# A cross-attention kernel's first microseconds: warm-up on ones from VectorE, first key weights in two halves

## The chip, the cores and the metric

The kernel runs on one core of a Trainium2 chip. The metric is the device time of one execution in microseconds. The core's engines are named as the profile names them: PE is TensorE's matmul part and PEld its weight loads, DVE is VectorE, ACT is ScalarE, POOL is GpSimd, SP is SyncE, and the names with a q (SPq, ACTq) are the queues on which an engine issues its DMAs.

## The reference

The layer updates 128 latent rows of width 256 in three steps, each added to x: cross-attention to 12544 context rows (16 heads of 64), self-attention with low-rank additions, and a linear layer on rows rounded to fp8. Nearly all work is in the first.

```python
def _L0_xattn_ref(latents, context, ln_l_w, ln_l_b, ln_c_w, ln_c_b, Wq, Wkv, Wo, bo):
    lat = layernorm(latents, ln_l_w, ln_l_b)
    ctx = layernorm(context, ln_c_w, ln_c_b)
    q = (lat @ Wq).reshape(b, n, H, D).transpose(0, 2, 1, 3)
    kv = ctx @ Wkv
    k, v = jnp.split(kv, 2, axis=-1)
    ...
    attn = jnp.einsum('bhnd,bhsd->bhns', q, k) * scale
    attn = jnp.clip(attn, -11.0, 11.0)
    attn = jax.nn.softmax(attn, axis=-1)
    out = jnp.einsum('bhns,bhsd->bhnd', attn, v)
    ...
    return out @ Wo + bo

x = x + _L0_xattn_ref(_layernorm(x, axis=-1), ctx_1024, ...)
x = x + _L0_attn_ref(_layernorm(x, axis=-1), ...)
x = x + _L0_ffn_ref(_layernorm(x, axis=-1), ...)
```

## The kernel before

The 12544 context rows are worked in 49 pairs of 128-row tiles, and the 16 heads in two passes of 8, so the middle of the kernel is twice 49 pairs. For each tile TensorE computes the scores of 8 heads from the context (transposed in its layout, its first column subtracted) and weights into which query, key weights and the layer norm's scale are folded, then the values, then the weighted sum. fp32 accuracy comes from pairs of a high and a low part (three matmuls each, lines 463 to 465). ScalarE takes exponentials and makes high parts, VectorE clips, makes low parts and adds denominators, GpSimd computes the roots for the norms.

Every engine runs its own list of instructions; order across engines is set by hand with semaphores, and each engine's list is in program order. A DMA is issued from SP's or ACT's list and raises its semaphore by 16 when it has landed.

The head, which the change touches, goes as follows.

- SP issues its loads in the order of lines 325 to 337: x, the second chunk of the first half of Wk, the first context pair, the first half of Wq, the first transposed pair, the second pair (lines 312 and 317), the second half of Wq, the first half of Wv, pairs three and four, the second half of Wk.
- ACT issues the column constants (line 799) and the first chunk of Wk's first half (line 800, 256 KB, semaphore wk_half0_loaded).
- POOL makes the identity (lines 402 and 403), then small constants, and later, behind the roots of the first three pairs, the row of ones, the square of ones `ones_sq` (line 429), a head mask and the ones of `av`. All raise `s_const`, on whose count others wait.
- DVE waits for the identity and the columns, makes the folding matrix `foldT` (lines 1092 to 1097), then the layer norm of x (to line 1104, which writes `lat`), then statistics and differences of the first pairs.
- TensorE waits for the identity, runs `keep_warm(9)`, nine fp32 matmuls of the identity with itself whose results nobody reads (line 566; the trace shows each fp32 matmul as two passes), then waits for foldT and for the first chunk of Wk and folds it (`key_fold`, line 533), transposes `lat` (line 576), folds the second chunk, computes the queries from Wq (`q_heads`, line 548), and goes on to the query-key products (line 555) and the first scores (line 463).

`ones_sq` is read otherwise only by `denominators`, where a tile's denominators are summed by query, at the end of each pass; in pass two TensorE waited for `s_const` of 4 ahead of it.

Of the kernel before, what the change touches and what calls it, by code (L numbers as in the profile page):

```python
# [17 lines left out]
P = 128  # L18
# [5 lines left out]
def perceiver_layer(  # L24
    nc, x, ctx, ctxT, cols, Wq, Wk, Wv, Wo, bo,
    aWq, aAq, aBq, aWk, aAk, aBk, aWv, abv, aAv, aBv, aWo, abo, aAo, aBo,
    f_weight, f_scale, f_bias, out,
):
    _, N, D = x.shape
    PAIRS = ctx.shape[0]  # L30
    H, DH = Wo.shape[1], Wo.shape[0]
# [14 lines left out]
    CM = MH // CH  # L46
# [9 lines left out]
    with ExitStack() as stack:  # L56
        def sb(name, shape, dt=F32):
            return stack.enter_context(nc.sbuf_tensor(name, shape, dt))

        def sem(name):  # L60
            return stack.enter_context(nc.semaphore(name))
# [3 lines left out]
        bank = [wide[n // 2][:, n % 2, :] for n in range(8)]  # L65
# [8 lines left out]
        ident = sb("ident", [P, P])  # L74
# [5 lines left out]
        wkv = sb("wkv", [P, 2, PASSES, KD, IH])  # L80
# [22 lines left out]
        ones_sq = sb("ones_sq", [P, P])  # L103
# [57 lines left out]
        s_wk = [sem(f"wk_half{n}_loaded") for n in range(PASSES)]  # L161
# [2 lines left out]
        s_wo = sem("wo_loaded")  # L164
        s_late = sem("late_weights_loaded")
        s_const = sem("pool_constants_ready")
        s_dstep = sem("dve_step_done")
        s_pstep = sem("pool_step_done")
        s_var = sem("variance_ready")
# [139 lines left out]
        def _(sp):  # L309
# [10 lines left out]
            def sigma_row(gp_slot, i):  # L320
                for b in range(2):
                    sp.dma_start(diff[gp_slot][0:1, 0, b * P:(b + 1) * P], sig_all[:, bass.ds(2 * i + b, 1)],
                                 allow_slow_non_contiguous=True).then_inc(s_row[gp_slot], 16)

            sp.dma_start(x_sb[:, :], x_rows).then_inc(s_x, 16)
            sp.dma_start(wkv[:, 0, 0, :, CM * P:2 * CM * P], Wk[:, 0, :, CM * P:2 * CM * P]).then_inc(s_wkc, 16)
            sp.dma_start(x_pair[0][:, :, :], ctx[0, :, :, :]).then_inc(s_xin[0], 16)
# [65 lines left out]
        def _(pool):  # L393
            steps = [0]

            def const_step(ins):
                steps[0] += 1
                ins.then_inc(s_pstep, 1)
                pool.wait_ge(s_pstep, steps[0])
# [26 lines left out]
            ctx_rstd(1, 1, 1, 1)  # L426
            ctx_rstd(2, 0, 2, 2)
            pool.memset(ones_row[:, :], 1.0).then_inc(s_const, 1)
            pool.memset(ones_sq[:, :], 1.0).then_inc(s_const, 1)
            const_step(pool.memset(head_mask[:, :], 1.0))  # L430
            const_step(pool.affine_select(out=head_mask[:, :], in_=head_mask[:, :], compare_op=ALU.is_ge, fill=0.0,
                                          base=0, pattern=[[-AD, HT]], channel_multiplier=1))
# [27 lines left out]
        def _(pe):  # L460
# [50 lines left out]
            def denominators(dst, by_head, c):  # L511

                for h in range(c * HC, (c + 1) * HC):
                    ins = pe.matmul(dst[:, h * DW:(h + 1) * DW], by_head[:, h, :], ones_sq[:, 0:DW], start=(h == 0),  # L514
                                    stop=(h == HP - 1))
                if c == CH - 1:
                    ins.then_inc(s_denp, 1)
# [11 lines left out]
            def key_fold(half, ms, dst):  # L529

                for n, m in enumerate(ms):
                    for k in range(KD):
                        ins = pe.matmul(dst[:, n * D:(n + 1) * D], wkv[:, 0, half, k, m * P:(m + 1) * P], foldT[:, k, :],  # L533
                                        start=(k == 0), stop=(k == KD - 1))
                ins.then_inc(s_wkEp, 1)
# [27 lines left out]
            def keep_warm(n):  # L563

                for _ in range(n):
                    pe.matmul(bank[6][:, 0:P], ident[:, :], ident[:, :], start=True, stop=True)  # L566


            pe.wait_ge(s_const, 1)
            keep_warm(9)  # L570
            pe.wait_ge(s_foldT, 1)
            pe.wait_ge(s_wk[0], 16)
            key_fold(0, CHUNK_M[0], KEY_BANK[0])
            pe.wait_ge(s_latn, 1)
            for k in range(KD):
# [41 lines left out]
            def pair(p, i, phase):  # L617
                gp = p * PAIRS + i
                static = isinstance(i, int)
                for b in range(2):  # L620
# [40 lines left out]
                            pe.wait_ge(s_qklo, 2 * KD * CH)  # L661
                        value_fold(1, n, side_bank)
                    if p == 1 and extra == DEN_STEP:
                        pe.wait_ge(s_const, 4)
                        pe.wait_ge(s_wvlo, KD * PASSES)
                        for c in range(CH):
                            denominators(side_bank, den[0], c)
                    if p == 1 and extra in WO_STEPS:
# [7 lines left out]
                        project(0, h // 2, h % 2, side_bank[:, h % 2 * D:(h % 2 + 1) * D])  # L676

            passes(pe, pair)


# [116 lines left out]
        @block.scalar  # L797
        def _(act):
            act.dma_start(col_all[:, :], cols).then_inc(s_cols, 16)
            act.dma_start(wkv[:, 0, 0, :, 0:CM * P], Wk[:, 0, :, 0:CM * P]).then_inc(s_wk[0], 16)  # L800

            act.wait_ge(s_const, 2)
            act.activation(warm[:, :], neg_half[:, 0:1], ACT.Exp)
# [159 lines left out]
            effective_weights(3)  # L963
            self_exp(0)
            act.wait_ge(s_avp, 1)
            act.wait_ge(s_const, 6)
            act.copy(av[:, 0:AH, 0:AD], bank[1][:, 0:D].rearrange("p (h d) -> p h d", h=AH)).then_inc(s_av, 1)
            for n in range(1, 4):
                self_exp(n)
# [9 lines left out]
        def _(dve):  # L979
            count = [0]  # L980

            def link(ins):
                count[0] += 1
                ins.then_inc(s_dstep, 1)
                dve.wait_ge(s_dstep, count[0])
# [101 lines left out]
                ctx_veps(n, n % 2)  # L1087


            dve.wait_ge(s_const, 1)  # L1090
            dve.wait_ge(s_cols, 16)
            link(dve.tensor_scalar(neg_w[:, :], ctx_w[:, :], -1.0 / D, None, ALU.mult))
# [156 lines left out]
            dve.tensor_copy(identb[:, :], ident[:, :])  # L1249
            dve.wait_ge(s_hTp, 1)  # L1250
            dve.tensor_copy(hT[:, :, :], bank[4][:, 0:D].rearrange("p (k q) -> p k q", k=KD)).then_inc(s_hT, 1)
            dve.wait_ge(s_const, 5)
            link(dve.tensor_reduce(par_mask[:, :], head_mask[:, :].rearrange("p (j a) -> p a j", a=2), AX_X, ALU.add))
            for m in range(KD):
                dve.wait_ge(s_akp, 1)
# [107 lines left out]
```

## Time and profile before

| | us |
|---|---|
| median of 3 runs | 1068.64 |
| lowest and highest | 1068.26, 1068.66 |
| the profiled execution | 1069.05 |
| its span in the trace | 1067.3 |
| TensorE busy in the span | 1060.7 (99%) |
| VectorE, ScalarE, GpSimd busy | 928.1, 660.9, 173.7 |

The span is the stretch that the trace covers; 1.75 us of the profiled execution lie outside it. Starts in the timeline are counted from the span's beginning. The granted clock over the whole span is 0.999 of full speed. A timeline line gives start and duration, engine, line of the kernel, operation, written tile, read tiles, shape and count; where a line merges several instructions, the duration reaches from the first's start to the last's end. Matmuls overlap, so their durations are longer than the distance from one to the next.

### The profile page before, as it was taken

The numbers are of one execution on the slowest core, as the hardware profiler recorded it, in microseconds if no ns is written. First come the engines' busy times: TensorE is split into PE (matmuls) and PEld (weight loads), VectorE is DVE, ScalarE is ACT, GpSimd is POOL, SyncE is SP. The second block draws the span as 40 slices with busy tenths as digits, with TensorE's granted clock in tenths as the row PEclk, the third lists the DMA queues.
The fourth block names the chain that finished last, engine by engine and source line by source line (L and its number), as shares of the span: only waits on it lengthen the run. The fifth ranks groups of instructions, "written<-read, shape, count | busy, mean of one in ns | idle before, by whom it ended". The sixth has DMA issues, their size and how long they took to land.

```text
span 1067.3 us, 18228 instructions
## 1 busy us (share of the span) xinstructions
PE 1060.7 (99%) x5503; PEld 901.3 (84%) x5503; DVE 928.1 (87%) x1328; ACT 660.9 (62%) x934; POOL 173.7 (16%) x214
## 2 busy tenths in 40 slices
PE   9999999999999999999999999999999999999998
PEld 7888888888888888888888888888888888888886
DVE  4999999999999999988888888888888888888875
ACT  4666666666666666656666666666666666656642
POOL 3232332332322323312000000000000000000000
PEclk9999999999999999999999999999999999999999
DMA  5312212212222122122151111111111111111000
GB/s 202 95 51 73 74 49 74 73 50 74 64 59 74 52 71 74 50 86 67 52 124 30 44 44 30 44 42 32 44 31 42 44 30 44 44 30 31 1 1 6
DMA packets 52909, 58.78 MB, mean 55 GB/s; under 512 B 31186, under 2 KB 33300, under 8 KB 52756
## 3 DMA queue, kind: packets, MB, share of 16 engines
q1 hardware_dynamic: 52324, 58.06, 18.6%
q10 hardware_dynamic: 560, 0.40, 0.1%
q8 instruction: 14, 0.23, 0.1%
q14 instruction: 11, 0.09, 0.0%
HBM read 58.20 MB, written 0.13 MB: 55 GB/s over the span
## 4 chain that ended last, share of the span: by engine, by line
PE 98%; DVE 1%; issue 0%; ACT 0%; POOL 0%; POOLq 0%; DVEq 0%
PE wide L463 25%; PE wide L464 25%; PE wide L465 25%; PE wide L504 17%; PE wide L533 1%; PE wide L526 1%; PE wide L540 1%; PE wide L555 1%; PE wide L566 0%; PE wide L548 0%; PE wide L514 0%; PE wide L521 0%; PE wide L767 0%; PE wide L561 0%; PE wide L750 0%
## 5 line engine op out<-in xcount | busy, mean ns | idle before, releaser
L839 ACT ACTIVATE ex<-wide,c_rstd 128x512 f32<-128x512 f32 x392 | 270.3, 689 | 199.5 <-PE wide L465 198.4
L463 PE MATMUL wide<-qk_hi,d_hi 128*128 128x512 f32 x784 | 305.3, 389 | 0.0
L465 PE MATMUL wide<-qk_hi,d_lo 128*128 128x512 f32 x784 | 305.0, 389 | 0.0
L464 PE MATMUL wide<-qk_lo,d_hi 128*128 128x512 f32 x784 | 305.0, 389 | 0.0
L1054 DVE TENSOR_TENSOR ph<-ex,ph 128x1024 fp32r<-128x1024 f32 x195 | 238.9, 1225 | 70.3 <-ACT ph L846 70.1
L846 ACT CAST ph<-ex 128x1024 fp32r<-128x1024 f32 x195 | 205.3, 1053 | 150.7 <-DVE ex L1027 150.7
L1063 DVE TENSOR_TENSOR den_all<-den_all,ex 128x1024 f32<-128x1024 f32 x193 | 234.6, 1215 | 0.0
L504 PEld LDWEIGHTS wide<-ph,vhl 128*128 128x128 f32 x1568 | 212.7, 190 | 16.6 <-DVE ph L1054 1.6
L504 PE MATMUL wide<-ph,vhl 128*128 128x256 f32 x1568 | 219.0, 282 | 0.0
L463 PEld LDWEIGHTS wide<-qk_hi,d_hi 128*128 128x128 f32 x784 | 147.2, 188 | 31.9 <-DVE qk_lo L1068 0.3
L465 PEld LDWEIGHTS wide<-qk_hi,d_lo 128*128 128x128 f32 x784 | 147.1, 188 | 30.6
L464 PEld LDWEIGHTS wide<-qk_lo,d_hi 128*128 128x128 f32 x784 | 147.2, 188 | 30.4
L1027 DVE TENSOR_SCALAR ex<-ex 128x1024 f32<-128x1024 f32 x195 | 135.1, 693 | 33.4 <-ACT ex L839 24.8
L463 PE MATMUL wide<-wv_hi,d_hi 128*128 128x512 f32 x392 | 158.0, 403 | 0.0
L464 PE MATMUL wide<-wv_lo,d_hi 128*128 128x512 f32 x392 | 154.7, 395 | 0.0
L465 PE MATMUL wide<-wv_hi,d_lo 128*128 128x512 f32 x392 | 152.7, 390 | 0.0
L1016 DVE SCALAR_TENSOR_TENSOR vhl<-wide,c_rstd,vhl 128x512 fp32r<-128x512 f32 x196 | 146.1, 745 | 3.1 <-ACT vhl L832 3.0
L832 ACT ACTIVATE vhl<-wide,c_rstd 128x512 fp32r<-128x512 f32 x196 | 133.5, 681 | 5.4 <-PE wide L465 5.0
L415 POOL TENSOR_TENSOR sig_all<-c_veps,half_pow 128x2 f32 (+1 forms) x49 | 45.9, 938 | 352.3 <-DVE c_veps L1007 352.3
L421 POOL COPY c_rstd<-rstd_all 128x2 f32 (+1 forms) x49 | 27.2, 555 | 458.5 <-ACT ex L839 458.5
L465 PEld LDWEIGHTS wide<-wv_hi,d_lo 128*128 128x128 f32 x392 | 73.7, 188 | 16.9
L463 PEld LDWEIGHTS wide<-wv_hi,d_hi 128*128 128x128 f32 x392 | 74.3, 190 | 10.8 <-issue 0.5
(163 smaller groups left out, 632.0 us busy)
## 6 DMA issues: line engine op xcount, KB each, us to landing
t_all<-in_ctxT_dram SPq DMA_DIRECT2D x98, 384.0 KB, 3.1
x_pair<-in_ctx_dram SPq DMA_DIRECT2D x49, 256.0 KB, 2.6
diff<-sig_all SPq DMA_DIRECT2D x194, 0.5 KB, 1.9
wkv<-in_Wo_dram SPq DMA_DIRECT2D x2, 1024.0 KB, 10.1
wq<-in_Wq_dram SPq DMA_DIRECT2D x2, 512.0 KB, 7.6
wkv<-in_Wv_dram SPq DMA_DIRECT2D x2, 512.0 KB, 6.3
wkv<-in_Wk_dram SPq DMA_DIRECT2D x1, 512.0 KB, 11.4
wkv<-in_Wk_dram SPq DMA_DIRECT2D x1, 256.0 KB, 3.5
```

Source lines behind the costliest of these rows:

```text
L415: pool.tensor_tensor(sig_all[:, pair_cols], c_veps[s][:, :], half_pow[:, :], ALU.pow).then_inc(s_sig, 1)
L463: pe.matmul(dst, hi, mhi, start=start, stop=False)
L464: pe.matmul(dst, hi, mlo, start=False, stop=False)
L465: return pe.matmul(dst, lo, mhi, start=False, stop=stop)
L504: ins = pe.matmul(acc[m][:, a, :, :], vhl[b][:, 2 * m + a, :, :].rearrange("p n d -> p (n d)"), ph[b][:, place(m, a), :, :], start=start a ...
L832: act.activation(vhl[b][:, :, 0, :], v_bank[:, :].rearrange("p (h d) -> p h d", h=HP), ACT.Identity, scale=c_rstd[s4][:, b:b + 1]).then_in ...
L839: act.activation(ex[b][:, c * HC:(c + 1) * HC, :], sc_bank[c][:, :].rearrange("p (h q) -> p h q", h=HC), ACT.Exp, scale=c_rstd[s4][:, b:b ...
L846: act.copy(ph[b][:, :, 0, :], ex[b][:, :, :]).then_inc(s_phi, 1)
L1016: dve.scalar_tensor_tensor(vhl[b][:, :, 1, :], v_bank[:, :].rearrange("p (h d) -> p h d", h=HP), c_rstd[s4][:, b:b + 1], vhl[b][:, :, 0, : ...
L1027: dve.tensor_scalar(ex[b][:, :, :], ex[b][:, :, :], EXP_LO, EXP_HI, ALU.max, ALU.min).then_inc(s_clip, 1)
L1054: dve.tensor_tensor(ph[b][:, :, 1, :], ex[b][:, :, :], ph[b][:, :, 0, :].bitcast(F32), ALU.subtract)\
L1063: dve.tensor_tensor(den[p], den[p], ex[b][:, :, :], ALU.add).then_inc(s_den, 1)
```

## The change

DVE writes the square of ones as its very first instruction and raises a semaphore of its own, and POOL's memset of it goes. TensorE's warm-up waits for that semaphore instead of the identity's, multiplies the ones with themselves and has 8 matmuls instead of 9; the wait for the identity comes behind it. The first chunk of Wk is loaded by partitions: 64 to 127 by SP, ahead of all its other loads, and 0 to 63 by ACT, where the whole was; TensorE waits for both. The counts of `s_const` are lowered by one where they were above the removed step, and the wait ahead of pass two's denominators goes.

```diff
+            sp.dma_start(wkv[DH:P, 0, 0, :, 0:CM * P], Wk[DH:P, 0, :, 0:CM * P]).then_inc(s_wk[0], 16)
             sp.dma_start(x_sb[:, :], x_rows).then_inc(s_x, 16)
...
             pool.memset(ones_row[:, :], 1.0).then_inc(s_const, 1)
-            pool.memset(ones_sq[:, :], 1.0).then_inc(s_const, 1)
...
                 for _ in range(n):
-                    pe.matmul(bank[6][:, 0:P], ident[:, :], ident[:, :], start=True, stop=True)
-
-
+                    pe.matmul(bank[6][:, 0:P], ones_sq[:, :], ones_sq[:, :], start=True, stop=True)
+
+
+            pe.wait_ge(s_ones, 1)
+            keep_warm(8)
             pe.wait_ge(s_const, 1)
-            keep_warm(9)
             pe.wait_ge(s_foldT, 1)
-            pe.wait_ge(s_wk[0], 16)
+            pe.wait_ge(s_wk[0], 32)
...
                     if p == 1 and extra == DEN_STEP:
-                        pe.wait_ge(s_const, 4)
                         pe.wait_ge(s_wvlo, KD * PASSES)
...
             act.dma_start(col_all[:, :], cols).then_inc(s_cols, 16)
-            act.dma_start(wkv[:, 0, 0, :, 0:CM * P], Wk[:, 0, :, 0:CM * P]).then_inc(s_wk[0], 16)
+            act.dma_start(wkv[0:DH, 0, 0, :, 0:CM * P], Wk[0:DH, 0, :, 0:CM * P]).then_inc(s_wk[0], 16)
...
-            act.wait_ge(s_const, 6)
+            act.wait_ge(s_const, 5)
...
+            dve.memset(ones_sq[:, :], 1.0).then_inc(s_ones, 1)
             dve.wait_ge(s_const, 1)
...
-            dve.wait_ge(s_const, 5)
+            dve.wait_ge(s_const, 4)
```

## Rows read from the trace of the kernel before

**Rows 1.** The page: busy shares, then the chain that ended last, by engine.

```profile
PE 1060.7 (99%) x5503; PEld 901.3 (84%) x5503; DVE 928.1 (87%) x1328; ACT 660.9 (62%) x934; POOL 173.7 (16%) x214
...
PE 98%; DVE 1%; issue 0%; ACT 0%; POOL 0%; POOLq 0%; DVEq 0%
```

**Rows 2.** The page, costliest groups: busy, mean ns of one, idle before and its releaser.

```profile
L839 ACT ACTIVATE ex<-wide,c_rstd 128x512 f32<-128x512 f32 x392 | 270.3, 689 | 199.5 <-PE wide L465 198.4
```

**Rows 3.** Timeline of all engines, 0 to 3.4 us: start, duration, what.

```profile
0.81 0.20 POOL L402 MEMSET ident<- 128x128 f32 x1 [0.29 <-POOLq L1322]
0.81 0.39 SPq L325 DMA_DIRECT2D x_sb<-in_x_dram  x1
...
1.25 0.29 POOL L403 TENSOR_SCALAR_AFFINE_SELECT ident<-ident 128x128 f32<-128x128 f32 x1 [0.23 <-POOL ident L402]
1.27 0.42 SPq L326 DMA_DIRECT2D wkv<-in_Wk_dram  x1
1.27 0.46 ACTq L800 DMA_DIRECT2D wkv<-in_Wk_dram  x1
...
1.60 4.21 PE L566 MATMUL wide<-ident 128*128 128x128 f32 x18 [1.60 <-POOL ident L403]
...
3.33 0.17 DVE L1092 TENSOR_SCALAR neg_w<-col_all 128x2 f32<-128x2 f32 x1 [3.33 <-DMA col_all<-in_cols_dram]
```

**Rows 4.** Timeline of PE, four narrow stretches (5.7, 5.8, 6.6, 8.1 us).

```profile
5.38 0.42 PE L566 MATMUL wide<-ident 128*128 128x128 f32 x1
...
5.79 0.77 PE L533 MATMUL wide<-foldT,wkv 128*128 128x256 f32 x1
...
6.34 0.63 PE L533 MATMUL wide<-foldT,wkv 128*128 128x256 f32 x1
...
7.62 0.81 PE L533 MATMUL wide<-foldT,wkv 128*128 128x256 f32 x3
```

**Rows 5.** Timeline of all engines, 3.8 to 6.5 us, VectorE's lines.

```profile
3.80 0.28 DVE L1094 TENSOR_SCALAR foldT<-ident,neg_w 128x128 f32<-128x128 f32 x1
...
4.44 0.16 DVE L1097 COPY foldT<-col_all 128x2 f32<-128x2 f32 x1
...
6.08 0.41 DVE L1104 TENSOR_SCALAR lat<-x_sb,mv,rstd 128x256 f32<-128x256 f32 x1 [0.74 <-POOL rstd L410]
```

**Rows 6.** ACT's DMA queue by stretch (3:4, 4:5, 5:6 us): packets, MB, engine share.

```profile
q10 hardware_dynamic: 142, 0.15, 41.2%
...
q10 hardware_dynamic: 119, 0.11, 33.2%
...
q10 hardware_dynamic: 6, 0.01, 1.5%
```

**Rows 7.** DMA issues by stretch (0.7 to 4.7 us): KB, us to landing.

```profile
x_sb<-in_x_dram SPq DMA_DIRECT2D x1, 128.0 KB, 2.2
...
wkv<-in_Wk_dram ACTq DMA_DIRECT2D x1, 256.0 KB, 4.4
...
wq<-in_Wq_dram SPq DMA_DIRECT2D x1, 512.0 KB, 6.8
...
t_all<-in_ctxT_dram SPq DMA_DIRECT2D x1, 384.0 KB, 8.0
...
wq<-in_Wq_dram SPq DMA_DIRECT2D x1, 512.0 KB, 8.4
```

**Rows 8.** Timeline of all engines, 8.4 to 17.1 us: PE's and VectorE's lines.

```profile
8.49 0.38 PE L576 MATMUL wide<-ident,lat 128*128 128x128 f32 x2
...
10.44 1.95 PE L548 MATMUL wide<-latT,wq 128*128 128x128 f32 x16
...
14.00 0.69 DVE L1011 TENSOR_TENSOR d_lo<-diff,d_hi 128x512 fp32r<-128x512 f32 x1 [1.38 <-ACT d_hi L826]
...
14.38 2.05 PE L548 MATMUL wide<-latT,wq 128*128 128x128 f32 x16
...
17.01 0.50 PE L463 MATMUL wide<-qk_hi,d_hi 128*128 128x512 f32 x1
```

More of the change, by code:

```diff
@@ L166, in perceiver_layer @@
         s_const = sem("pool_constants_ready")
+        s_ones = sem("ones_ready")
         s_dstep = sem("dve_step_done")
```

## The prediction

> **What bounds the kernel now.** I read the page's busy shares and chain first: TensorE is busy 99% of the span and the chain that ended last is 98% TensorE [rows 1]. The costliest group says the same from the other side: ScalarE's exponentials sit idle for 199.5 us, of which 198.4 us end with a matmul [rows 2]. So in the long middle of the kernel only TensorE's own work counts, and the change touches none of that work. What it can change is the time at which TensorE reaches the middle: a microsecond won in the first twenty is handed through one to one, because everything behind is queued on TensorE, and a microsecond lost likewise. The second view is therefore the timeline of the first microseconds [rows 3, 4], the third is DVE's timeline beside it [rows 5], and the last two are the DMA queues and landings [rows 6, 7].
>
> The head today goes like this. TensorE waits for POOL's identity, which is ready at 1.25 + 0.29 = 1.54 us, and starts its warm-up at 1.60 [rows 3]. It issues 18 passes (9 fp32 matmuls of two passes each); the last starts at 5.38 [rows 4] and passes follow each other at 3.78/17, near 0.22 us (0.213 in the steady part), so the engine is free for the next one at about 5.60. The first key fold starts at 5.79. What ended the gap is the load of Wk: issued by ACT at 1.27 [rows 3], landing 4.4 us later [rows 7], at 5.67; the fold's first pass starts 0.12 us after that. The other thing it needs, foldT, was ready at 4.44 + 0.16 = 4.60 [rows 5]. So today Wk binds, the warm-up is 0.07 us ahead of it, foldT more than a microsecond.
>
> The clock matters too. The profile's granted clock prints 1.00 over all of the head, but the passes say otherwise: the fold's passes of 256 columns start at 5.79, 6.34 and then every 0.427 us up to 7.62, and the next ones follow every 0.213 us, reaching the transposes at 8.49 [rows 4, 8]. That is a factor of two, the lower level (1.2 GHz) up to about 7.62 and the higher (2.4 GHz) behind it. TensorE had worked for 6.0 us, almost without a gap, when its rate rose.
>
> **The change part by part.**
>
> Ones in place of the identity. DVE, which did nothing before 3.33 us [rows 3], now writes the 128x128 ones. The trace has no DVE memset; the bounds are POOL's memset of a tile of that size, 0.20 us [rows 3], and DVE's 128x128 tensor_scalar, 0.28 us [rows 5]. The engines' queues begin at 0.81 us [rows 3], so the ones are ready at 1.01 to 1.09; TensorE started 0.06 us after its releaser before, so now at 1.07 to 1.15. I take 1.10: the warm-up begins 0.50 us sooner. DVE's next step waits for the column constants until 3.33 anyway, so the memset costs DVE nothing; if the columns came before 1.1 us, it would cost its full 0.28.
>
> One warm-up matmul less: two passes, 0.43 us. The warm-up is through at 1.10 + (5.60 - 1.60) - 0.43 = 4.67 us.
>
> Wk in halves. Each queue now carries 128 KB of it: SP as its first load, ACT behind the columns as before. The x load shows what 128 KB first on SP's queue takes: 2.2 us from 0.81, about 3.0 [rows 7]. For ACT's half: its queue moved 142 packets in the span's fourth microsecond, 119 in the fifth, 6 in the sixth [rows 6], nearly all of them Wk's kilobyte packets (256 in all). Half of those, 128, fit into the fourth microsecond; with the same half microsecond from the last packets to the landing (about 5.2 to 5.67) it lands near 4.5. The bounds: 4.3 (half of the way from 3.0, where the queue's packets set in densely, to 5.67) and 5.21 (only the 0.46 us by which the first half's issue moves, below). The fold now starts behind the latest of foldT 4.60, warm-up 4.67 and Wk 4.5: at about 4.8 with the same 0.12 us. That is 1.0 us sooner than 5.79, range 0.45 to 1.1. What binds is then a near tie of all three.
>
> SP's queue moves back. Each SP issue takes 0.39 to 0.46 us of the queue [rows 3], so x, the second key chunk, Wq and the context pairs are issued about 0.43 us later. x lands at 3.0 + 0.43 and is used by DVE only behind foldT at 4.6: free. The bytes ahead of each later load are the same as before, since Wk's half went through ACT's queue earlier on. So those loads land between 0 and 0.43 us later. The first Wq half lands at 2.24 + 6.8 = 9.04 today and would at 9.04 to 9.47; its matmuls begin at 10.44 [rows 7, 8], and 0.12 us behind the landing would be 9.16 to 9.59. This is what is late next. The second Wq half lands at 4.57 + 8.4 = 12.97, then up to 13.40, used at 14.38 [rows 7, 8]. The second pair's transposed context lands at 3.79 + 8.0 = 11.79, then up to 12.22; DVE's difference (0.69) follows and stands ahead of d_lo, which starts at 14.00 [rows 8], so it is done by 13.0. All three hold for a gain up to 0.85 us.
>
> The rate. Eight passes of the first fold lie across its rise. Had it been at one rate throughout, the gain would be the whole 1.0 or nothing; so three cases. (a) The rise keeps its distance to the first warm-up pass (6.02 us): it comes at 7.12. Pass starts 4.80, 5.35, 5.78, 6.21, 6.63, 7.06, then 7.30 and 7.51, and the transposes at 7.72 instead of 8.49: 0.77 us. (b) It stays at 7.62: starts 4.80 to 7.49 at the slow pitch, one more at 7.80, transposes at 8.02: 0.47 us. (c) It comes by 4.8, since the engine is now loaded from 1.10 instead of 1.60: eight passes end at 6.6, behind lat, which is ready at 6.08 + 0.41 = 6.49 [rows 5]; transposes and second fold take 1.95 us (8.49 to 10.44 [rows 8]) and end at 8.6, where Wq holds TensorE until 9.16 to 9.59: 0.85 to 1.28 us.
>
> The rest. The memset of ones leaves POOL at a time when POOL waits anyway, one wait leaves TensorE's tail of pass one, and the counts of the constants are renumbered: nothing. The multiplied data has no reader. If TensorE had waited on POOL there, there would be something to gain; the chain shows no such share.
>
> **Two rules of the Trainium skill.** The trace shows ACT's queue and SP's sharing the same stretch, 142 packets in 1 us for the one [rows 6] while the other went on. The Trainium skill (DMA: Bandwidth & Descriptors, section Issuing engines are not separate DMA queues) says that loads issued from several engines run on the same 16 DMA engines and that this saves only the issuing time; that speaks against the split. By it alone Wk would come just its 0.46 us earlier, which is the third rival below. The trace agrees that the DMA engines are shared; it doesn't show a split load. On the rate, the Trainium skill (TensorE: Matmul & The Clock Gate, section Part 1: The HAM clock gate) says that where the rise falls differs from run to run of one kernel; by it cases (a) to (c) could all appear, and the profile after would be one draw. The three times before agree within 0.40 us, which bounds such a scatter here.
>
> **The sum.** 1.0 us at the start of the fold, less 0.23 for the passes at the slow rate: 0.77, of which I keep 0.7, because Wq, the warm-up and foldT each come within 0.1 us of binding. The profiled execution took 1069.05 us for a span of 1067.3, so the forecast is a span of 1066.6 and 1068.35 us for such an execution. It stood 0.41 above the median of the three, 1068.64; against the median the forecast is 1067.9 us.
>
> **The rivals.**
> 1. The rise stays where it is (b): 1068.64 - 0.47 = 1068.2 us. For it: nothing in the trace ties the rise to the first pass. Chance 0.23.
> 2. The rise comes early (c): the gain is cut by Wq, 1067.4 to 1067.8 us. For it: TensorE is now loaded half a microsecond longer before any given time; against it: before, 6.0 us of load went by ahead of the rise. Chance 0.20.
> 3. The halves land only as much sooner as SP's first issue: Wk at 5.21, the fold at 5.33. With the rise at 7.12 the transposes start at about 8.03, with 7.62 at 8.24: gain 0.25 to 0.46, 1068.2 to 1068.4 us. For it: the same bytes on the same DMA engines; against: the queue's packets by microsecond. Chance 0.12.
> 4. The change doesn't do what it says: the ACT half lands as late as the whole did, because SP's loads crowd it, or the start of Wq cancels the gain: 1068.5 to 1068.7 us. Chance 0.07.
> 5. Slower, by a lost rise. With one warm-up matmul less, the warm-up ends at 4.67; if Wk came only at 5.67, TensorE would stand idle for a microsecond just before its rate is due to rise. If that put the rise off past the first two folds, the stretch from 7.62 to 10.44 would run at half the rate and take 2.8 us more: 1071.5 us. It decides from the point at which Wk lands later than about 5.2, and it needs the gap to count. Chance 0.03.
>
> **How the numbers follow.** The forecast (a) has 0.35, and the five rivals 0.23, 0.20, 0.12, 0.07 and 0.03. The range 1067.2 to 1068.85 holds all of them but the fifth, with 0.2 us of the runs' own spread on either side; it is left wide by the landings (0.45 to 1.1) and by the rise. A measurement of this kernel can tell about 0.2%, 2.1 us, from no change. No case of gain reaches that: even with everything free at once Wq's landing stops it at 1.28. So faster 0.01, within 0.2% 0.96, slower 0.03.
>
> **What would show it.** In the profile after: the first L566 pass near 1.1 us on DVE's ones (if at 1.6, the first step is wrong); 16 passes; the first fold pass near 4.8 (5.3 is rival 3, 5.8 rival 4); the place where the fold's pitch goes from 0.427 to 0.213 us (7.1 is (a), 7.6 rival 1, before 4.8 rival 2, past 10 rival 5); the Wq matmuls near 9.7 with their load landed before; and the first score matmuls (17.01 before [rows 8]) near 16.3. The prediction fails if something in the middle, not TensorE, turns out to hold the end, so that a head gain doesn't arrive.

## The result and the profile after

The changed kernel takes 1069.73 us (median of 21 runs, 1069.19 to 1071.56), the kernel before 1068.44 (21 runs beside it, 1067.83 to 1069.08): 1.29 us more, ratio 1.0013, 95% interval 1.0007 to 1.0019. The forecast was 0.7 us less. The change is inside the 0.2% that was named as no change, but it is clear of the noise and on the other side.

The page of the changed kernel's profiled execution (1069.8 us, close to its median) has these busy shares and this chain that ended last (span 1068.1 us):

```profile
PE 1059.8 (99%) x5501; PEld 899.9 (84%) x5501; DVE 928.6 (87%) x1329; ACT 660.6 (62%) x934; POOL 173.6 (16%) x213
...
PE 97%; DVE 1%; DMA 1%; issue 0%; SPq 0%; ACT 0%; DVEq 0%
```

Against [rows 1] the chain has a new member, "DMA 1%": TensorE waited for a load, and the chain runs through that load from its issue to its landing, which is more than the wait itself. The timeline of all engines, 0 to 17.5 us (start, duration, what, and in brackets the idle time before it with its releaser), shows which; it answers to [rows 3, 4, 5, 8]:

```profile
0.81 0.77 SPq L326 DMA_DIRECT2D wkv<-in_Wk_dram  x1
...
0.91 0.17 DVE L1091 MEMSET ones_sq<- 128x128 f32 x1 [0.91 <-PEq L1324]
...
1.13 3.78 PE L567 MATMUL wide<-ones_sq 128*128 128x128 f32 x16 [1.13 <-DVE ones_sq L1091]
...
1.25 0.73 ACTq L801 DMA_DIRECT2D wkv<-in_Wk_dram  x1
...
1.64 0.57 SPq L327 DMA_DIRECT2D x_sb<-in_x_dram  x1
...
3.27 0.43 SPq L330 DMA_DIRECT2D wq<-in_Wq_dram  x1
...
4.87 1.97 PE L534 MATMUL wide<-foldT,wkv 128*128 128x256 f32 x8
4.93 0.43 DVE L1101 BATCH_NORM_STATS2 stats<-x_sb 128x6 f32<-128x256 f32 x1 [0.99 <-DMA x_sb<-in_x_dram]
...
6.50 0.41 DVE L1106 TENSOR_SCALAR lat<-x_sb,mv,rstd 128x256 f32<-128x256 f32 x1 [0.74 <-POOL rstd L412]
...
6.97 0.44 PE L578 MATMUL wide<-ident,lat 128*128 128x128 f32 x2
...
7.25 1.89 PE L534 MATMUL wide<-foldT,wkv 128*128 128x256 f32 x8
...
10.79 2.05 PE L549 MATMUL wide<-latT,wq 128*128 128x128 f32 x16 [1.65 <-DMA wq<-in_Wq_dram]
...
14.83 2.05 PE L549 MATMUL wide<-latT,wq 128*128 128x128 f32 x16
...
17.46 0.50 PE L464 MATMUL wide<-qk_hi,d_hi 128*128 128x512 f32 x1
```

The first half of what was wanted is there (the rate, below, is the pitch at which matmul passes follow each other; its rise is the change from the slow pitch to the fast one). The ones are ready at 1.08, the warm-up starts at 1.13 instead of 1.60, and the first fold starts at 4.87 instead of 5.79, all eight passes at the fast pitch (1.97 us for eight instead of 2.87). The second fold starts at 7.25 instead of 8.71. Then TensorE stands for 1.65 us, until Wq is there, and the Wq matmuls start at 10.79, 0.35 later than before. The first scores are 0.45 later (17.46 for 17.01).

Why Wq is late stands in the SP and ACT rows. The half of Wk took SP 0.77 us to issue, not the 0.39 to 0.46 of the loads in [rows 3]; ACT's half took 0.73; x, next on SP's queue, took 0.57. Wq is issued at 3.27, 1.03 later than the 2.24 of before. The DMA issues of the same kernel, by stretch (KB, us from issue to landing; answers to [rows 7]):

```profile
wkv<-in_Wk_dram SPq DMA_DIRECT2D x1, 128.0 KB, 3.1
...
wkv<-in_Wk_dram ACTq DMA_DIRECT2D x1, 128.0 KB, 3.5
x_sb<-in_x_dram SPq DMA_DIRECT2D x1, 128.0 KB, 3.3
...
wq<-in_Wq_dram SPq DMA_DIRECT2D x1, 512.0 KB, 7.5
```

SP's half lands at 3.9, ACT's at 1.25 + 3.5 = 4.75, x at 4.9 instead of 3.0 (so `lat` is ready at 6.91, 0.42 later, and the transposes start right behind it, at 6.97), and Wq at 3.27 + 7.5 = 10.77 instead of 9.04.

From there the delay is handed through the middle unchanged. ScalarE's exponential of the same tile, in the timeline of ACT near 500 us, first before:

```profile
500.74 0.69 ACT L839 ACTIVATE ex<-wide,c_rstd 128x512 f32<-128x512 f32 x1
```

and after:

```profile
501.19 0.69 ACT L840 ACTIVATE ex<-wide,c_rstd 128x512 f32<-128x512 f32 x1
```

That is 0.45 us, at 17 us as at 501. But the spans differ by 0.8 us. The other part arises at one place in the tail, where VectorE waits for the self-attention's keys. The timeline of all engines from 1040 to 1047 us, before:

```profile
1042.51 1.95 PE L697 MATMUL wide<-latT,x_pair 128*128 128x128 f32 x16
...
1044.57 0.90 DVE L1256 SCALAR_TENSOR_TENSOR den_all<-wide,col_all,par_mask 128x256 f32<-128x256 f32 x2 [2.22 <-PE wide L697]
```

and after:

```profile
1042.96 1.95 PE L698 MATMUL wide<-latT,x_pair 128*128 128x128 f32 x16
...
1045.39 0.88 DVE L1258 SCALAR_TENSOR_TENSOR den_all<-wide,col_all,par_mask 128x256 f32<-128x256 f32 x2 [2.60 <-PE wide L698]
```

VectorE starts 2.06 us behind the start of the matmuls that it waits for in the one, 2.43 us in the other, though nothing around it was edited. Behind it the offset is 0.74 us instead of 0.45. So the profiled executions show a loss in the head, 0.45, and one in the tail, 0.29. The medians show 1.29 us. The other half microsecond is that the profiled execution of before was 0.61 above its own median (1069.05 against 1068.44).

### The profile page after: what moved, and what is told of

Its sections match the earlier page's. It is cut to its first block, busy times and chain, and to the rows that moved or that the text cites. A ratio compares the mean times of both kernels' runs of the same rounds, so it can differ in the third digit from the quotient of the medians.

```text
span 1068.1 us, 18224 instructions
## 1 busy us (share of the span) xinstructions
PE 1059.8 (99%) x5501; PEld 899.9 (84%) x5501; DVE 928.6 (87%) x1329; ACT 660.6 (62%) x934; POOL 173.6 (16%) x213
## 4 chain that ended last, share of the span: by engine, by line
PE 97%; DVE 1%; DMA 1%; issue 0%; SPq 0%; ACT 0%; DVEq 0%
PE wide L464 25%; PE wide L465 25%; PE wide L466 25%; PE wide L505 17%; DMA wq<-in_Wq_dram 1%; PE wide L527 1%; PE wide L541 1%; PE wide L556 1%; PE wide L549 0%; PE wide L515 0%; PE wide L768 0%; PE wide L534 0%; PE wide L562 0%; PE wide L522 0%; PE wide L751 0%
```

## The experiments

The times are medians of 11 runs of the experiment and, beside it, of 27 or 33 runs of the kernel before on the same chip, taken alternately. How much of an offset arises in the head and how much in the tail (behind 1043 us) is read from the timelines as above. Executions of one kernel differ in when the rate rises and when the loads land; each traced one is called a draw.

### The kernel before once more

> The kernel before, once more, for a second draw of its trace. Theory D (draw): its profiled execution (span 1067.3, TensorE's rate rising at 7.62 us) was a late draw; in another the rise comes elsewhere between about 4.8 and 8 us, and where it is earlier the Wq matmuls start before 10.44, at best 9.16, and the span is shorter by the same amount, up to 1.2 us: 1066.1 to 1067.3. The changed kernel's loss is then 0.74 us by the two spans and up to 0.6 more by the medians because the profiled execution of before was a slow one. Rival: the rise is fixed by the kernel and comes at 7.6 again, span 1067.3 within 0.1; then the medians' 1.29 us hide a cost outside the span.

Measured: 1068.32 us (1067.62 to 1068.96) beside 1068.22. Its timeline:

```profile
6.15 2.44 PE L533 MATMUL wide<-foldT,wkv 128*128 128x256 f32 x8 [0.34 <-DMA wkv<-in_Wk_dram]
...
10.38 1.95 PE L548 MATMUL wide<-latT,wq 128*128 128x128 f32 x16
```

Here Wk landed later (5.97 instead of 5.67), the fold started at 6.15, and its eight passes took 2.44 us instead of 2.87: the pitch changed earlier. The draw came out nearly as late as the first, span 1067.2; but its runs reach from 1067.62 to 1068.96, and this profiled execution was the slowest of them. Two variants below with the head of before (one and four VectorE memsets added) give the fast draw: fold at 5.46 and 5.37 with all passes fast, Wq matmuls at 9.21 and 9.12. So the time at which the Wq matmuls start in the kernel before should be anything between 9.1 and 10.4, and theory D holds: my forecast compared against the late end. No fast execution of the kernel before itself was traced; the fast end is taken from the two variants.

### The two parts apart

Only the split load, with the warm-up of before:

```diff
+            sp.dma_start(wkv[DH:P, 0, 0, :, 0:CM * P], Wk[DH:P, 0, :, 0:CM * P]).then_inc(s_wk[0], 16)
...
-            act.dma_start(wkv[:, 0, 0, :, 0:CM * P], Wk[:, 0, :, 0:CM * P]).then_inc(s_wk[0], 16)
+            act.dma_start(wkv[0:DH, 0, 0, :, 0:CM * P], Wk[0:DH, 0, :, 0:CM * P]).then_inc(s_wk[0], 16)
```

> The kernel before with only the split load: halves by partitions, SP's half first; the warm-up is that of before, on the identity, 9 matmuls from 1.60 us. Theory S: SP's issue of the half takes 0.77 us, all its other loads move back, Wq lands at 10.6 and its matmuls start near 10.8 as in the changed kernel, 0.3 to 1.6 us later than before: time 1069.0 to 1069.7. Theory T: no second loss behind 1044 us, since VectorE's list is that of before. Rival W (the warm-up did the harm): Wq matmuls near 10.4 or earlier and time 1068.4.

Measured: 1069.12 us (1068.60 to 1069.72) beside 1068.22, 0.90 more; ratio 1.0009 (1.0000 to 1.0018). The profiled execution (1068.60) was the fastest of the eleven:

```profile
0.81 0.76 SPq L325 DMA_DIRECT2D wkv<-in_Wk_dram  x1
...
5.60 2.52 PE L534 MATMUL wide<-foldT,wkv 128*128 128x256 f32 x8
5.62 0.43 DVE L1100 BATCH_NORM_STATS2 stats<-x_sb 128x6 f32<-128x256 f32 x1 [1.77 <-DMA x_sb<-in_x_dram]
...
9.91 1.95 PE L549 MATMUL wide<-latT,wq 128*128 128x128 f32 x16
```

SP's issue takes 0.76, and x is there only at 5.6: VectorE's statistics stand 1.77 us for it and start at 5.62 (4.51 before). But TensorE waits for neither x nor Wq in this draw: Wq lands at 3.28 + 6.0 = 9.3, not at the 10.6 of the expectation, and its matmuls start at 9.91 behind a fold that begins at 5.60, where the warm-up ends, and takes 2.52 us. So theory S has its time (forecast 1069.0 to 1069.7), and the late issue is in the trace, but which wait costs the 0.9 us of the median isn't shown by this kernel; the traces of the changed kernel show it at Wq. Theory T holds: without the memset there is no second loss in the tail (2.05 us from the matmuls' start to VectorE's, as before).

Only the ones and the shorter warm-up, with the load of before:

> The changed kernel without the split load: the warm-up on VectorE's ones and the renumbered waits, Wk's first chunk whole on ACT's queue. Theory S (SP's queue does the harm): Wk lands at 5.67 as before, Wq at 9.04; the warm-up ends at 4.9, TensorE idles 0.9 us, the fold starts at 5.8, and the time is that of the kernel before within 0.4 us (1068.0 to 1068.8), but for the tail. Theory T (tail): the 0.29 us that the changed kernel loses once more behind 1044 us belongs to VectorE's list of instructions, which is one longer; it shows here too, and the time is 0.3 above before. Rival W: the shorter warm-up costs, by a gap ahead of the rate's rise: rise past 8.5 us, 1069.5 and more.

Measured: 1068.64 us beside 1068.22, but the eleven runs fall into groups: five from 1067.65 to 1067.89, two near 1068.66, four from 1070.26 to 1070.73. The profiled execution was of the fast group (Wk landed at 5.07 there):

```profile
5.17 2.05 PE L533 MATMUL wide<-foldT,wkv 128*128 128x256 f32 x8 [0.25 <-DMA wkv<-in_Wk_dram]
...
9.01 1.95 PE L548 MATMUL wide<-latT,wq 128*128 128x128 f32 x16
```

Here the fold starts at 5.17 and Wq is waited for by nobody. The upper group is taken up below. Theory T holds (2.43 us in the tail), and rival W holds for four runs of eleven. Theory S has its median, by some luck since it lies between two groups; Wk landed 0.6 us sooner than it said.

### The form of the split, and what stands ahead

The changed kernel with halves by input block, each 128 partitions of one row:

```diff
-            sp.dma_start(wkv[DH:P, 0, 0, :, 0:CM * P], Wk[DH:P, 0, :, 0:CM * P]).then_inc(s_wk[0], 16)
+            sp.dma_start(wkv[:, 0, 0, 1, 0:CM * P], Wk[:, 0, 1, 0:CM * P]).then_inc(s_wk[0], 16)
...
-            act.dma_start(wkv[0:DH, 0, 0, :, 0:CM * P], Wk[0:DH, 0, :, 0:CM * P]).then_inc(s_wk[0], 16)
+            act.dma_start(wkv[:, 0, 0, 0, 0:CM * P], Wk[:, 0, 0, 0:CM * P]).then_inc(s_wk[0], 16)
```

> The changed kernel with the halves cut by the block of 128 input rows instead of by partitions: each half has 128 partitions of one 1 KB row, the shape of the x load, instead of 64 partitions of two. Theory P (partition shape): the 0.77 us issue belongs to the 64-partition form; here SP's first issue takes 0.39 to 0.45 us, SP's other loads stand 0.4 instead of 1.03 us behind those of before, Wq lands near 9.5 instead of 10.66, and the time falls to 1068.0 to 1068.6 (with the tail's 0.3). Rival Q (any load ahead): whatever its shape, a load ahead of the others pushes them back; Wq lands at 10.5 or later and the time stays at 1069.5 or more.

Measured: 1068.86 us (1068.49 to 1069.19) beside 1068.22, 0.64 more. The timeline's rows and the DMA issue of Wq:

```profile
0.81 0.39 SPq L326 DMA_DIRECT2D wkv<-in_Wk_dram  x1
...
2.71 0.43 SPq L330 DMA_DIRECT2D wq<-in_Wq_dram  x1
...
5.00 3.02 PE L534 MATMUL wide<-foldT,wkv 128*128 128x256 f32 x8
...
wq<-in_Wq_dram SPq DMA_DIRECT2D x1, 512.0 KB, 6.5
```

The issue takes 0.39, Wq is issued at 2.71 and lands at 9.21. Theory P holds for the issue and the landing; the time is 0.26 above its range. By the medians about half of the 1.2 to 1.3 us is the form with 64 partitions; whether through its issue alone or also through its transfer (SP's half took 3.0 to 3.3 us to land in that form, 2.5 and 2.6 in this) the runs don't separate. What is left is not nothing. With the ones written by POOL instead, which takes the tail's loss out, the same split was run again:

> The split load by blocks (each half 128 partitions, SP's half first) with the ones written by POOL, so that VectorE's list is that of before and the tail's 0.28 us are not in it. Theory S: what is left is the cost of a 128 KB load ahead of SP's others, 0.36 us by subtraction (1068.86 less 0.28 less 1068.22): median 1068.5 to 1068.7 where the kernel before takes 1068.2 to 1068.4. Rival: the split by blocks costs nothing or gains, median 1068.2 or less.

Measured: 1068.63 us (1068.13 to 1068.89) beside 1068.31, 0.32 more (ratio 1.0002, 0.9993 to 1.0011). Its timeline shows two waits for loads:

```profile
5.50 1.97 PE L535 MATMUL wide<-foldT,wkv 128*128 128x256 f32 x8 [0.71 <-DMA wkv<-in_Wk_dram]
...
9.94 2.05 PE L550 MATMUL wide<-latT,wq 128*128 128x128 f32 x16 [0.52 <-DMA wq<-in_Wq_dram]
```

The 0.32 is near the 0.36 by subtraction, though the interval includes no change at all. In both medians a 128 KB load ahead of SP's others costs about a third of a microsecond more than the earlier Wk gives; in this draw Wk itself wasn't early (5.4), and Wq, issued 0.47 late, was waited for again.

### Does Wq's landing hold the changed kernel?

> The changed kernel again, for a second draw of its trace. Theory S: its typical execution waits for Wq. In this draw too the Wq matmuls begin right behind the load of Wq (10.0 to 10.9 us) and TensorE is idle ahead of them, wherever the rate rises; time 1069.4 to 1069.9, spread of most executions under 1 us. Rival D: the late landing (7.4 us behind the issue) was chance; here Wq lands 6.0 to 6.5 us behind its issue at 3.27, the matmuls begin where TensorE gets to them, and the loss of the median comes from executions in which the rate rose late.

Measured: 1069.40 us (1068.40 to 1069.78) beside 1068.20.

```profile
4.79 2.66 PE L534 MATMUL wide<-foldT,wkv 128*128 128x256 f32 x8
...
10.09 2.05 PE L549 MATMUL wide<-latT,wq 128*128 128x128 f32 x16 [0.69 <-DMA wq<-in_Wq_dram]
...
14.52 2.05 PE L549 MATMUL wide<-latT,wq 128*128 128x128 f32 x16 [0.31 <-DMA wq<-in_Wq_dram]
```

Another draw of the rate (eight passes in 2.66 us instead of 1.97), another landing (6.8 us behind the issue instead of 7.5), and again both halves of Wq are waited for: 0.69 us ahead of the first, 0.31 ahead of the second. So theory S holds. The better of two draws by 0.7 us at the first Wq matmul is better by only 0.3 at the scores.

The exchange of Wq and the first context pair:

```diff
-            sp.dma_start(x_pair[0][:, :, :], ctx[0, :, :, :]).then_inc(s_xin[0], 16)
             sp.dma_start(wq[:, 0, :, :], Wq[:, 0, :, :]).then_inc(s_wq[0], 16)
+            sp.dma_start(x_pair[0][:, :, :], ctx[0, :, :, :]).then_inc(s_xin[0], 16)
```

> The changed kernel with one exchange in SP's order: the first half of Wq ahead of the first context pair, which nobody needs before 11 us. Theory S: Wq now lands 1 to 1.5 us sooner (issue 2.76 instead of 3.27, 256 KB less ahead of it), about 9.2 to 9.5; TensorE no longer waits for it, and the median falls by 0.5 to 1.0, to 1068.7 to 1069.2. Rival: if Wq's landing isn't what costs, the median stays at 1069.5 or more.

Measured: 1069.98 us beside 1068.20, 0.6 more than the changed kernel there. The expectation was wrong, and the rows say why:

```profile
9.91 2.05 PE L549 MATMUL wide<-latT,wq 128*128 128x128 f32 x16 [0.62 <-DMA wq<-in_Wq_dram]
10.54 0.75 DVE L1001 BATCH_NORM_STATS2 c_stats<-x_pair 128x6 f32<-128x256 f32 x2 [3.64 <-DMA x_pair<-in_ctx_dram]
...
12.93 0.60 PE L588 MATMUL wide<-ident,sig_all 128*1 128x128 f32 x4 [0.96 <-POOL sig_all L417]
```

Wq did come sooner (9.9), though not at the 9.2 to 9.5 expected, and TensorE still waited 0.62 us for it. The context pair now lands at 10.5, and from it VectorE's statistics and POOL's roots take until 12.9; TensorE waits 0.96 us for them. I had written that nobody needs the pair before 11 us; TensorE is ready for its roots at 12.93 - 0.96 = 11.97, and with the 2.4 us from landing to roots that is a landing by about 9.6. Behind Wq the next wait was already standing.

### The tail

The kernel before with one memset more at the head of VectorE's list, then with four:

```diff
+            dve.memset(y[:, :], 1.0)
             dve.wait_ge(s_const, 1)
             dve.wait_ge(s_cols, 16)
```

> The kernel before with one instruction more at the head of VectorE's list, a memset of a tile of 128x256 that is overwritten later; nothing else. Theory T: the 0.28 us lost behind 1044 us come from the length of VectorE's list, so this kernel loses them too: offset of the tail 0.28 larger than that of the body, median 1068.5 against 1068.2. Rival: they come from something else of the change (the wait taken from TensorE's list, the POOL step, the counts of the constants); then the tail's offset equals the body's and the median is 1068.2.

Measured: 1068.48 us beside 1068.20; the interval of the ratio includes no change (0.9994 to 1.0012), so the trace has to carry it.

```profile
5.46 1.97 PE L533 MATMUL wide<-foldT,wkv 128*128 128x256 f32 x8
...
9.21 1.95 PE L548 MATMUL wide<-latT,wq 128*128 128x128 f32 x16
...
1041.16 1.95 PE L697 MATMUL wide<-latT,x_pair 128*128 128x128 f32 x16
...
1043.59 0.88 DVE L1257 SCALAR_TENSOR_TENSOR den_all<-wide,col_all,par_mask 128x256 f32<-128x256 f32 x2 [2.60 <-PE wide L697]
```

2.43 us from the matmuls' start to VectorE's, as in the changed kernel. With four (on disjoint quarters of the tile):

> The kernel before with four small memsets at the head of VectorE's list (disjoint parts of a tile that is overwritten later) where one memset moved the tail's offset by 0.28 us. Theory P (position): the loss hangs on where the waiting instruction at 1044 us falls in VectorE's list; with four more it falls elsewhere, and the tail's offset minus the body's is 0 or another value than 0.28. Theory N (number): each instruction more costs; the tail loses 0.28 times four or the same 0.28. Median 1068.2 if the loss is gone, 1068.5 if it is the same, 1069.3 if it is fourfold.

Measured: 1068.23 us beside 1068.36.

```profile
1041.17 1.95 PE L697 MATMUL wide<-latT,x_pair 128*128 128x128 f32 x16
...
1043.23 0.88 DVE L1260 SCALAR_TENSOR_TENSOR den_all<-wide,col_all,par_mask 128x256 f32<-128x256 f32 x2 [2.22 <-PE wide L697]
```

2.06 us, as before, and no loss. That rules out theory N in both its forms and fits theory P, that it hangs on where the waiting instruction falls in VectorE's list. Over all traces the split is clean: 2.43 us in the seven with one VectorE instruction more, 2.05 or 2.06 in the ten with none or four. Why one position is slower the traces don't show; that stays open.

### The idle stretch ahead of the rise

The kernel before with 7, then 5 warm-up matmuls instead of 9, and the ones-only kernel with 10 instead of 8; one number each in the call of `keep_warm`.

> The kernel before with 7 warm-up matmuls instead of 9, from 1.60 us: they end near 4.75 and TensorE is idle for 0.4 to 1.2 us until Wk lands. Theory W (an idle stretch ahead of the rise can lose the rise): some executions, a quarter to a half, take 2 to 2.7 us more and form a group of their own at 1070.2 and above; the others stay at 1067.4 to 1069.0. Rival: idle time there costs nothing since Wk isn't there; all executions are between 1067.4 and 1069.0.

Measured: 1069.69 us beside 1068.36; five runs from 1067.68 to 1068.84, one at 1069.69, five from 1070.38 to 1070.74. The profiled one (1068.22) is of the fast group:

```profile
5.45 2.36 PE L533 MATMUL wide<-foldT,wkv 128*128 128x256 f32 x8 [0.50 <-DMA wkv<-in_Wk_dram]
```

> The ones-only kernel (VectorE writes the ones, Wk's first chunk whole on ACT's queue), which took 1068.64 with 4 of 11 executions at 1070.3 to 1070.7, with 10 warm-up matmuls instead of 8 and nothing else. Theory W: the upper group is gone, executions from 1067.9 to 1068.7, median near 1068.3: the POOL-written version's 1068.02 plus the tail's 0.28. Theory T: tail offset 0.28 above the body's. Rival: the group stays, so the idle stretch isn't what makes it.

Measured: 1068.28 us (1067.92 to 1068.96) beside 1068.36; no upper group.

> The kernel before with 5 warm-up matmuls instead of 9. They end near 3.9 us and TensorE is idle for 1.2 to 1.8 us until Wk lands. With 7 (idle 0.4 to 1.2) 5 of 11 executions were at 1070.4 to 1070.7, but no profiled execution was among them. Theory W: now most executions are in the upper group, the profiled one probably too, and its trace shows the fold's passes at the pitch of 0.427 us to the end and the rise past 8 us, the Wq matmuls near 11.5 to 12; median 1070 to 1071. Rival: the upper group comes from elsewhere; its share stays at a half or less and the rise comes before 8 us.

Measured: 1069.84 us (1069.10 to 1070.86) beside 1068.31: no run is as fast as the median of before. The forecast was too high all the same: only three of eleven runs lie above 1070.2, and the median is below 1070. This time the profiled execution (1069.91) is one of the late ones:

```profile
5.61 3.75 PE L533 MATMUL wide<-foldT,wkv 128*128 128x256 f32 x8 [1.51 <-DMA wkv<-in_Wk_dram]
...
11.29 1.95 PE L548 MATMUL wide<-latT,wq 128*128 128x128 f32 x16
```

Behind 1.51 us without a matmul the fold's eight passes take 3.75 us, nearly all at the slow pitch, and the Wq matmuls start at 11.29. It is what the prediction's fifth rival describes, at a smaller price: 1.5 us against before's median here, about 2.3 in the upper groups, 2.8 forecast.

So theory W holds for the length of the warm-up: 9 to 7 matmuls makes an upper group, 8 to 10 removes it, 5 puts all runs above the median of before. The length of the idle stretch alone doesn't tell the executions apart. TensorE was idle for 0.34 us in the kernel before's second trace, for 0.37 in the one with 10 matmuls on VectorE's ones and for 0.71 in the block split with 8 matmuls on POOL's ones (its row is above), and none of these three kernels has an upper group; in the last two the fold's passes were all fast, so the rate had risen by then. A shorter warm-up is both less work and a longer idle time, which the runs don't separate, and only the kernel with 5 has a trace of a late execution.

The changed kernel itself doesn't suffer from it as a rule, since Wk lands at 4.65 to 4.75 in its two traces and leaves a gap of under 0.2 us; one of its 21 runs, at 1071.56, lies where such a run would lie, without a trace to show it.

### Versions that should be better

Ones by POOL as its first instruction, 10 warm-up matmuls, the load of before (against the changed kernel; VectorE's memset and SP's half of Wk go as well):

```diff
+            pool.memset(ones_sq[:, :], 1.0).then_inc(s_ones, 1)
             const_step(pool.memset(ident[:, :], 0.0))
...
             pe.wait_ge(s_ones, 1)
-            keep_warm(8)
+            keep_warm(10)
```

> A version that keeps the part that may pay: ones written by POOL as its first instruction (VectorE's list is that of before), 10 warm-up matmuls from about 1.1 to 5.5 us, Wk's first chunk whole on ACT's queue. With 8 such matmuls and an idle stretch of 0.3 to 0.9 us ahead of the fold, 4 of 11 executions took 1070.3 to 1070.7. Theory W (a gap ahead of the rise can lose the rise): with the gap closed none or one of the executions is above 1069.5; the rate rises up to 0.5 us sooner, median 1067.7 to 1068.1. Theory T: body and tail offset are the same. Rival to W: the gap has nothing to do with it, and about a third of the executions is at 1070.3 again.

Measured: 1068.02 us (1067.69 to 1068.34) beside 1068.20.

```profile
5.41 1.97 PE L534 MATMUL wide<-foldT,wkv 128*128 128x256 f32 x8 [0.19 <-DMA wkv<-in_Wk_dram]
...
9.16 1.95 PE L549 MATMUL wide<-latT,wq 128*128 128x128 f32 x16
```

> The POOL-written ones with 10 warm-up matmuls and the unsplit load once more, since its first comparison (ratio 0.9997, interval 0.9988 to 1.0006) left open whether it beats the kernel before. Theory W with the earlier start: all executions below 1068.5, median 0.1 to 0.4 below before. Rival: the first result was chance; median equal to before within 0.1.

Measured: 1068.01 us (1067.80 to 1068.66) beside 1068.31. The median is where it was expected, but two runs are above 1068.5. Both times the ratio is 0.9997 (0.9988 to 1.0006): 0.2 and 0.3 us ahead of before by the medians, with the slow draws mostly gone, but not shown to be faster.

To that, the second chunk of Wk on ACT's queue:

```diff
-            sp.dma_start(wkv[:, 0, 0, :, CM * P:2 * CM * P], Wk[:, 0, :, CM * P:2 * CM * P]).then_inc(s_wkc, 16)
...
+            act.dma_start(wkv[:, 0, 0, :, CM * P:2 * CM * P], Wk[:, 0, :, CM * P:2 * CM * P]).then_inc(s_wkc, 16)
```

> The kernel of the POOL-written ones and 10 warm-up matmuls (median 1068.02, Wq issued by SP at 2.24 and landing 6.3 us later), with the second chunk of Wk issued by ACT behind the first instead of by SP. SP's other loads are issued 0.45 us sooner; the bytes are the same. Theory I (the issue sets the landing): Wq lands 0.4 us sooner, near 8.1, the context pair too, and the median falls by up to 0.3, to 1067.7 to 1067.9. Rival B (the bytes ahead and the DMA engines' rate set it): Wq lands at 8.5 again or later, median 1068.0 to 1068.3.

Measured: 1069.39 us beside 1068.36.

```profile
1.72 0.42 SPq L328 DMA_DIRECT2D wq<-in_Wq_dram  x1
1.75 0.49 ACTq L801 DMA_DIRECT2D wkv<-in_Wk_dram  x1
...
9.38 1.99 PE L533 MATMUL wide<-foldT,wkv 128*128 128x256 f32 x8 [1.45 <-DMA wkv<-in_Wk_dram]
```

Wq, issued at 1.72, landed 6.4 us later at 8.1, as theory I had it; but the chunk on ACT's queue, issued at 1.75, took 7.6 us (3.8 on SP's queue, in the kernel without this edit), 1.45 of them with TensorE idle. The theory was right on the load I watched and the time wrong, because the wait moved to the load that I had moved.

## Why the prediction was wrong

**What held.** TensorE bounds, and a head offset goes through the middle one to one (0.45 at 17 us and at 501 us). Warm-up from 1.13 (1.10 forecast), Wk's halves at 3.9 and 4.75, the fold at 4.87 (4.8 forecast). The memset took 0.17 us, just under my bounds of 0.20 to 0.28. The near tie of three that I forecast ahead of the fold wasn't one: the column constants came sooner, foldT was ready at 3.95 instead of 4.60.

**The step that failed first: SP's queue moves back.** I took the half's issue at the 0.39 to 0.46 of [rows 3], rows of loads with 128 partitions; it was 0.77, x's behind it 0.57, and Wq's issue came 1.03 later, not 0.43. I then let the landings move by 0 to 0.43; x's moved by 1.9, Wq's by 1.7 and, in the second draw, 1.0. The reason that I gave, the same bytes ahead of each load, didn't keep x from taking 3.3 us instead of 2.2 and Wq from taking 7.5 instead of 6.8 behind the half. With Wq landing at 10.77 and 10.07 instead of at 9.04 to 9.47, TensorE stood idle for 1.65 and 0.69 us: the overlap that I counted on was gone, and with it the gain. The sentence "all three hold for a gain up to 0.85 us" left 0.1 us above the 0.77 of the sum, and an unseen form of instruction was priced as a seen one. This term, the split, was put at no cost and is 0.9 us by the median of the kernel that has it alone: some 0.3 to 0.4 for the load ahead of the others, the rest for its form.

**The second: "the memset costs DVE nothing".** It costs nothing where it stands, and 0.28 us a millisecond later. Together with the split, 0.90 + 0.28 is 1.18 of the measured 1.2 to 1.3.

**The third: the execution compared against.** My 0.7 us were to be won against Wq matmuls at 10.44. The timelines of the same head reach 9.1 to 9.2; there Wq lands at 8.9 and 8.4, which leaves about 0.2 and 0.6 us. A typical execution lies between. In the ten traces without the tail's loss the time is 1051.96 to 1052.12 us more than the start of the first scores, and the Wq matmuls start 6.57 ahead of the scores where nothing is waited for between them, so before's median of 1068.44 stands for Wq matmuls near 9.8. That is an estimate from these traces; with it, a Wq that is usable at my 9.16 to 9.59 would have allowed 0.2 to 0.7 us at most. I had the sign for it: the profiled time was 0.41 above the median of three, and I had bounded the scatter by three runs (0.40 us), where 21 runs spread over 1.25. This step makes the gain too large; it doesn't turn it into a loss.

**The rate.** The profiled execution was case (c), the rise ahead of the fold; the second draw, with 2.66 us for its eight passes, lies between (c) and (a). Case (c) has TensorE wait for Wq, and it did, but until 10.79 and not 9.16 to 9.59.

**The rivals.** The third and fourth had a late Wk, and Wk wasn't late. The fifth names a mechanism that a shorter warm-up brings out in three other kernels, but not the one that made this kernel slower; my point of decision, Wk past about 5.2, isn't borne out, since the block split on POOL's ones had Wk at 5.4 and no slow group. The fourth had the start of Wq cancel the gain, and stopped at zero. No rival said what happened: that a queue moved back costs more than the load moved to its head gives. The parts of it stood in my text as things that would hold, not as a rival.

**The rules weighed.** The Trainium skill (DMA: Bandwidth & Descriptors, section Issuing engines are not separate DMA queues) speaks against expecting more than issuing time from a second queue. The pair of traces that I compared differs: Wk landed 0.9 us sooner (4.75 for 5.67) with an issue moved by 0.46. All traces together agree with it: whole, Wk's first chunk landed at 5.1 to 6.0, in halves by partitions at 4.65 to 5.45, some 0.4 to 0.5 sooner at either end. Where a chunk moved to ACT's queue, Wq landed 0.4 us sooner with its issue moved by 0.5, issuing time and nothing more; that the chunk itself then took 7.6 us the rule doesn't say. The Trainium skill (TensorE: Matmul & The Clock Gate, section Part 1: The HAM clock gate) has the rise vary from run to run; the trace agrees, with 1.97 and 2.66 us for the same eight passes of the same kernel. I had quoted it and still taken one execution as the base.

## What to carry to other kernels

A load put at the head of a queue moves all that stands behind it, so look up who waits for each of those and by how much they are early; and price an issue only from rows of the same shape (64 partitions took 0.77 us here, 128 took 0.39 to 0.46). When a gain is smaller than a microsecond, take the base from a median and from more than one trace, since one execution can sit 0.6 us off. Fill the wait ahead of TensorE's first real matmul to its end: a warm-up that is two matmuls too short cost 2 to 2.5 us in four and in five of eleven executions.

## What the runs showed of the hardware

- Issuing a load of 64 partitions with two 1 KB rows each took 0.76 to 0.77 us on SP and 0.73 on ACT; 128 partitions with one such row took 0.39 on SP.
- Where TensorE's rate rose differed from execution to execution: the passes change from 0.427 to 0.213 us at about 7.6 us in the first trace of before, and ahead of 5.4 in the fastest with its head. The granted clock column prints 1.00 over all of it.
- Warm-up length with the unsplit load: with 9 matmuls on the identity or 10 on the ones, executions lie within 1.9 us (before) and 1.1 us of each other; with two fewer, four and five of eleven form a group 2.0 to 2.5 us above before's median; with 5, all eleven are above it, by 0.8 to 2.5. The idle time in the traced executions (0.25, 0.50 and 1.51 us in these three kernels, but also 0.34 to 0.71 in kernels without such a group) doesn't by itself decide it.
- One instruction more in VectorE's list made a wait a millisecond later end 0.37 us later (2.43 for 2.06, in all seven traces with it); four more didn't.
- Two 256 KB loads in a row on ACT's queue, with SP's queue full, landed 4.1 and 7.6 us behind their issue (one trace); two in a row on SP's queue took 3.2 to 5.4 us in the traces that have them.
